# Sorting edges by one-hot products in PSUM instead of GpSimd's scatter through DRAM, in a four-layer graph network

## The chip, the cores and the metric

The kernel runs on one core of a Trainium2 chip. The metric is the time of one execution in device microseconds (us); lower is better. A profile comes from one execution of its own.

## What is computed

A graph with 3125 nodes (32 features) and 53,125 directed edges, each with a source, a destination, a type (20 of them) and 16 attributes. Four layers follow, each on the layer norm of x with a ReLU, each added to x:

```python
def reference(x, src, dst, edge_attr_16, edge_type_20, ...):
    h = relu(layernorm(x)); x = x + rel(rel(h))       # two relational layers, a relu between
    h = relu(layernorm(x)); x = x + segment_sum(h[src], dst)
    h = relu(layernorm(x)); x = x + flow(h)
    h = relu(layernorm(x)); return x + attention(h)    # softmax over each node's incoming edges

def rel(h):   # message of an edge: h[src] @ W[type], W[type] = sum of 8 basis matrices
    return segment_sum(message, dst) + h @ w_loop + bias
def flow(h):  # past = src, future = dst
    fwd = mlp_f(concat(h[future], h[past], edge_attr))   # one row for each edge
    bwd = mlp_b(concat(h[past], h[future], edge_attr))
    return mlp_n(concat(segment_sum(fwd, future), segment_sum(bwd, past)))
```

## The kernel before

**Order of the edges.** Nodes lie in 25 blocks of 128 (NB). The kernel sorts the edges by block of their destination into 440 tiles (T) of 128 slots; each tile belongs to one block, so slots stay empty at the end of a block. All layers then go over the 440 tiles.

**Sorting (sort_edges, L183 to L430)** is three blocks of code with a barrier between them. The first (L194 to L341): the edges are loaded as 125 partitions x 425 columns (EP, EC); DVE makes a mask and a running count for each block (L274 to L291), TensorE (PE) adds up counts over partitions (for which DVE waits before L291), DVE works out each edge's slot (L291 to L327). SP loads dst, src, type, then all edge attributes, then the inputs of the relation weights. GpSimd (POOL) makes constants, clears `records` and makes the weights of layer 1 (make_weights, L502 and L504). The second block (L344 to L412) goes over the 425 columns: ScalarE (ACT) copies the records of five columns to a buffer, DVE their row numbers, and GpSimd issues one indirect DMA for each column (L362), which writes 125 records of 20 floats to the DRAM tensor `sorted_edges`. Five buffers of five columns are in flight. Beside it, on the other engines, runs `table_stage` of layer 1 (L510 to L574): layer norm, 25 transposes, and for each block of nodes two products with the weights of all relations (L570) into two PSUM banks, copied by DVE (L547) and ACT (L557) and written to the table `message_table` of 62,500 rows (node, relation) by SP (L529). Two pairs of banks take turns. The third block (L414 to L430) loads `sorted_edges` back (4400 KB) and derives indices (L427 to L430).

**Relational passes.** For each of the two layers a pass goes over the tiles in steps of eight: DVE copies eight index columns (L609), GpSimd gathers eight tiles of rows from the message table (L598), DVE makes one-hot matrices, PE adds up (L630). Between them stands `table_stage` of layer 2.

**Sum layer** (sum_layer, L743) and its gathers (L798).

**Flow layer** (flow_layer, from L953). Four tiles (G) in a step, 110 steps, five buffers (BUFS), written as a loop of 22 rounds with five steps unrolled. In each step GpSimd waits for one index copy of DVE (L1017) and issues four gathers of node rows of 128 bytes (L1002); DVE makes one-hot matrices (L1019, L1024) and masked messages (L1045); ACT copies the attributes and the flag of the step's slots out of `records` into the last 17 columns of X (L1060), beside other copies; PE turns X (L1112, after it has waited for the gathers and the copy), runs the two small networks, and adds up forward (L1136) and backward messages (L1139). A step's buffer is handed back when PE is through with it.

**Attention** takes the last stretch, with 440 gathers of rows of 256 bytes (L1357); PE L1490 and ACT L1437 hand turned scores over.

## Time and profile before

| | |
|---|---|
| time, median of 3 runs | 4871.88 us (4849.11 to 4895.27) |
| span of the profiled execution | 4857.7 us |
| PE busy | 2328.2 us (48%) |
| DVE busy | 1913.1 us (39%) |
| ACT busy | 475.2 us (10%) |
| POOL busy | 2571.2 us (53%) |
| HBM read, written | 54.41 MB, 27.29 MB |

The profiled execution is one of its own: its span is the time from its first to its last instruction, and the run's time has some us around it. Busy shares are means over stages with different limits, so they say little on what sets the end; the stages have to be read one by one.

### The profile page before, as it was taken

How to read it: one execution, taken by the hardware profiler on the slowest of the kernel's cores; microseconds unless marked ns; L12 is line 12 of the kernel's file. 1: busy time of each engine (PE TensorE's matmuls, PEld its weight loads, DVE VectorE, ACT ScalarE, POOL GpSimd, SP SyncE). 2: the span in 40 equal slices, each digit the busy share in tenths (PEclk: the TensorE clock that was granted, in tenths of full speed). 3: DMA queues.
4: the chain of work that ended last, by engine and by line, in shares of the span. 5: the costliest groups of instructions: out<-in, count | busy, mean ns of one | idle time of the engine just before them, and what ended most of it. 6: DMA issues, size and time to landing. Idle time of an engine off the chain costs nothing. (4 is left out here: it accounts for less than half of the span.)

```text
span 4857.7 us, 64843 instructions
## 1 busy us (share of the span) xinstructions
PE 2328.2 (48%) x20169; PEld 1793.5 (37%) x20302; DVE 1913.1 (39%) x6164; ACT 475.2 (10%) x1072; POOL 2571.2 (53%) x2544
## 2 busy tenths in 40 slices
PE   1300002332363232335556489888888455565562
PEld 0100002333343332334555355555555344344441
DVE  8000001111121111144545466665665455555557
ACT  0000000000000000000000022222222111111110
POOL 4777775666626666644554444444443444444440
PEclk9555555555555555555656699999998556656655
DMA  3211111000020000010000100000000000000010
GB/s 89 62 7 7 7 7 48 12 11 12 11 72 12 11 11 12 12 19 14 15 15 14 12 9 8 8 8 7 8 7 5 19 15 15 16 14 16 15 15 4
DMA packets 122759, 82.94 MB, mean 17 GB/s; under 512 B 75092, under 2 KB 109016, under 8 KB 122456
## 3 DMA queue, kind: packets, MB, share of 16 engines
q0 software_dynamic: 80160, 46.17, 8.2%
q1 hardware_dynamic: 42552, 36.17, 2.6%
q8 instruction: 27, 0.44, 0.0%
q14 instruction: 20, 0.16, 0.0%
HBM read 54.41 MB, written 27.29 MB: 17 GB/s over the span
## 5 line engine op out<-in xcount | busy, mean ns | idle before, releaser
L598 POOL DMA_INDIRECT rel_rows<-message_table,rel_index x880 | 842.5, 957 | 519.0 <-issue 277.0
L630 PE MATMUL rel_acc<-rel_rows,rel_onehot 128*128 128x32 f32 x1760 | 393.6, 372 | 872.4 <-issue 582.9
L630 PEld LDWEIGHTS rel_acc<-rel_rows,rel_onehot 128*128 128x128 f32 x1760 | 402.5, 324 | 863.5 <-issue 863.2
L1002 POOL DMA_INDIRECT flow_x<-node_table,flow_index x440 | 424.6, 965 | 548.5 <-DVE flow_index L1017 440.4
L1357 POOL DMA_INDIRECT att_kv_rows<-kv_table,att_index x440 | 421.0, 957 | 508.9 <-DVE att_index L1368 380.3
L362 POOL DMA_INDIRECT sorted_edges<-scatter_rows,scatter_index x425 | 505.4, 1189 | 131.7 <-issue 128.8
L1139 PE MATMUL flow_acc_bwd<-flow_onehot_j,flow_by_q 128*128 128x309 bf16 (+1 forms) x2508 | 557.5, 337 | 8.8 <-issue 0.4
L798 POOL DMA_INDIRECT sum_rows<-node_table,sum_index x320 | 326.3, 1020 | 295.1 <-DVE sum_index L821 195.6
L609 DVE COPY rel_index<-message_indices 128x8 uint32 x110 | 22.2, 202 | 1051.7 <-remote 956.1
L860 PE MATMUL p_sum_picked<-sum_h_parts,sum_source_onehot 128*128 128x96 bf16 x3000 | 250.6, 260 | 209.7 <-issue 204.1
L831 DVE TENSOR_SCALAR sum_source_onehot<-sum_sources,sum_node_numbers 128x384 bf16<-128x384 f16 x1000 | 235.7, 314 | 289.1 <-PE p_sum_picked L860 148.8
L1393 DVE TENSOR_REDUCE att_tile_max<-p_att_scores 128x4 f32<-128x512 f32 x440 | 282.4, 685 | 95.6 <-PE p_att_scores L1502 69.8
L860 PEld LDWEIGHTS p_sum_picked<-sum_h_parts,sum_source_onehot 128*128 128x128 bf16 x3000 | 217.1, 129 | 240.4 <-issue 233.1
L663 PE MATMUL rel_acc<-w_loop,h_transposed 33*128 33x32 f32 x100 | 21.7, 398 | 578.6 <-DMA w_loop<-in_L_gnn_b 578.6
L1499 PE MATMUL p_att_scores<-att_mask,identb 128*128 128x512 bf16 x440 | 231.5, 526 | 90.8 <-ACT att_parts_turned L1437 50.2
L1502 PE MATMUL p_att_scores<-att_parts_turned,att_pick 96*128 96x128 bf16 x1760 | 238.6, 277 | 4.3 <-issue 4.2
L1136 PE MATMUL flow_acc_fwd<-flow_messages,flow_onehot 128*128 128x32 bf16 x1320 | 235.8, 179 | 8.3 <-DVE flow_by_q L1045 8.3
L663 PEld LDWEIGHTS rel_acc<-w_loop,h_transposed 33*128 33x128 f32 x100 | 21.5, 329 | 580.5 <-DMA w_loop<-in_L_gnn_b 580.5
L396 DVE COPY scatter_index<-sorted_row 125x5 uint32 (+1 forms) x85 | 14.2, 171 | 535.4 <-DMA sorted_edges<-scatter_rows,scatter_index 535.1
L1502 PEld LDWEIGHTS p_att_scores<-att_parts_turned,att_pick 96*128 96x128 bf16 x1760 | 185.2, 126 | 101.4 <-issue 81.8
L1045 DVE TENSOR_TENSOR flow_by_q<-flow_messages,source_q_mask 128x512 bf16<-128x512 bf16 x330 | 207.3, 681 | 0.0
L1024 DVE TENSOR_SCALAR flow_onehot_j<-iota_j,source_j 128x821 bf16<-128x821 f16 x440 | 199.2, 453 | 0.0
(248 smaller groups left out, 3861.8 us busy)
## 6 DMA issues: line engine op xcount, KB each, us to landing
message_table<-message_rows SPq DMA_DIRECT2D x50, 320.0 KB, 2.1
rel_rows<-message_table,rel_index POOLq DMA_INDIRECT x880
flow_x<-node_table,flow_index POOLq DMA_INDIRECT x440
att_kv_rows<-kv_table,att_index POOLq DMA_INDIRECT x440
sorted_edges<-scatter_rows,scatter_index POOLq DMA_INDIRECT x425
sum_rows<-node_table,sum_index POOLq DMA_INDIRECT x320
sorted_edges<-records SPq DMA_DIRECT2D x1, 4400.0 KB, 12.0
records<-sorted_edges SPq DMA_DIRECT2D x1, 4400.0 KB, 13.1
```

The lines of the kernel that those rows point to most:

```text
L362: pool.indirect_dma_start(out=d["sorted"], out_offset=bass.IndirectOffsetOnAxis(ap=ibuf[g][:, c:c + 1], axis=0), in_=sbuf[g][:, c, :], in_ ...
L598: pool.indirect_dma_start(out=rows[b][:, t, :], out_offset=None, in_=table, in_offset=bass.IndirectOffsetOnAxis(ap=ibuf[b][:, t:t + 1], ax ...
L630: last = pe.matmul(acc[:, bass.ds(col, F)], hot[b][:, t, :], rows[b][:, t, :], start=False, stop=True, skip_group_check=True)
L798: pool.indirect_dma_start(out=rows[b][:, t, :], out_offset=None, in_=d["nodes"], in_offset=bass.IndirectOffsetOnAxis(ap=ibuf[b][:, t:t + 1 ...
L831: last = dve.tensor_scalar(which[b % 2][:, c, :], srcs[b][:], node[:, c:c + 1], None, ALU.is_equal)
L860: last = pe.matmul(pp[b % 2][:, t * 3 * F:(t + 1) * 3 * F], which[b % 2][:, c, t * P:(t + 1) * P], top(hpart[:])[:, :, c * F:(c + 1) * F], ...
L1002: pool.indirect_dma_start(out=X[b][:, t, 0:F], out_offset=None, in_=d["nodes"], in_offset=bass.IndirectOffsetOnAxis(ap=ibuf[b][:, t:t + 1] ...
L1136: pe.matmul(accF[:, bass.ds(col(b, t), F)], hot[b][:, t, :], top(M[b][:])[:, k, t, 0:F], start=False, stop=True, skip_group_check=True)
L1139: last = pe.matmul(accB[:, lo:hi], S[b][:, t, k, :], J[b][:, t, lo:hi], start=False, stop=True, skip_group_check=True)
L1357: pool.indirect_dma_start(out=KV[b][:, t, :], out_offset=None, in_=d["kv"], in_offset=bass.IndirectOffsetOnAxis(ap=ibuf[b][:, t:t + 1], ax ...
L1393: dve.tensor_reduce(tm[b][:, 0, t, :], pR[t % PR][:].rearrange("p (h e) -> p h e", h=HEADS), AX_X, ALU.max).then_inc(max_ready, 1)
L1502: last = pe.matmul(r[:, h, :], pick[:, t * HEADS + h, :], partT[b][:], start=False, stop=True, skip_group_check=True)
```

## The change

The sort no longer goes through DRAM. The first block now also holds the whole of `table_stage` of layer 1, with one pair of PSUM banks instead of two; ACT makes its transposed copies and both halves of its output copies, and PE runs it before the counts. The edge attributes are not loaded there, and `records` and `sorted_edges` are gone. DVE makes three numbers for each edge: the source (less 1562), destination in block and type in one (less 2048), and the edge's own number, written as the bits of an f16. In the second block DVE makes, for each of the 425 columns, a one-hot row over the 440 tiles (`at`) and three rows over the 128 slots that hold the carried number at the edge's slot (`put`); PE multiplies `put` and `at` and adds up over all columns in three PSUM banks, which then hold the three numbers of each slot. 15 DVE operations decode them. Sum and flow layer read `srcf` and `valid` instead of `records`. In the flow stage GpSimd also gathers each tile's edge attributes (rows of 64 bytes) from the input by the edge number, so there are eight gathers in a step, with a second index copy on DVE; ACT copies only the flag.

```diff
-SB = 5
+SB = 4
@@ sort_edges, first block
-                    sp.dma_start(stage[:, :, 0:FE], a["edge_attr_16"].rearrange("(p c) f -> p c f", p=EP))\
-                        .then_inc(staged, 16)
                     load_weights(sp)
-                    sp.dma_start(d["sorted"].rearrange("(p t) w -> p (t w)", p=P),
-                                 s["rec"][:].rearrange("p t w -> p (t w)")).then_inc(pads, 16)
+                    front["sp"](sp)
...
-                    pool.memset(s["rec"][:], 0.0).then_inc(recs, 1)
+                    pool.iota(number[:], pattern=[[1, EC]], base=0, channel_multiplier=EC).then_inc(numbered, 1)
                     make_weights(pool)
...
+                    front["act"](act)
+                    front["dve"](dve)
...
+                    v.done(dve.tensor_scalar(carried[0][:], src[:], float(-SRC_MID), None, ALU.add))
                     v.done(dve.tensor_scalar(tmp2[:], dst[:], P - 1, None, ALU.bitwise_and))
+                    v.done(dve.scalar_tensor_tensor(out=tmp[:], in0=tmp2[:], scalar=float(TYPES), in1=typ[:],
+                                                    op0=ALU.mult, op1=ALU.add))
+                    v.done(dve.tensor_scalar(tmp2[:], tmp[:], float(DT_MID), float(-DT_MID), ALU.is_ge, ALU.add))
+                    v.done(dve.tensor_tensor(carried[1][:], tmp[:], tmp2[:], ALU.add))
...
+                    front["pe"](pe)
                     pe.wait_ge(counts_ready, 1)
@@ sort_edges, second block
+                    for j in range(EC // SG):
+                        g = j % SB
+                        if j >= SB:
+                            dve.wait_ge(used, j - SB + 1)
+                        for i in range(SG):
+                            c = j * SG + i
+                            dve.tensor_scalar(at[g][:, i, :], iotahi[0:EP, :], hi[:, c:c + 1], None, ALU.is_equal)
+                            for k in range(3):
+                                last = dve.tensor_scalar(put[g][:, i, k, :], iotalo[0:EP, :], lo[:, c:c + 1],
+                                                         carried[k][:, c:c + 1], ALU.is_equal, ALU.mult)
+                        last.then_inc(made, 1)
...
+                    for j in range(EC // SG):
+                        g = j % SB
+                        pe.wait_ge(made, j + 1)
+                        for i in range(SG):
+                            for k in range(3):
+                                last = pe.matmul(sorted_[k][:, 0:T], put[g][:, i, k, :], at[g][:, i, :],
+                                                 start=(j == 0 and i == 0), stop=(j == EC // SG - 1 and i == SG - 1))
+                        last.then_inc(used, 1)
@@ table_stage
+    deep = 1 if layer == 1 else 2
-    py = [[ps(st, f"p_message{layer}{i}{j}", [P, BANK]) for j in range(2)] for i in range(2)]
+    py = [[ps(st, f"p_message{layer}{i}{j}", [P, BANK]) for j in range(2)] for i in range(deep)]
...
         for b in range(NB):
+            if layer == 1:
+                half_out(act, act.copy, b, 0)
+            half_out(act, act.copy, b, 1)
...
-            if b >= 2:
+            if b >= deep:
                 for j in range(2):
-                    pe.wait_ge(got[j], b - 1)
+                    pe.wait_ge(got[j], b - deep + 1)
@@ flow_layer
-                            pool.wait_ge(indexed, i * BUFS + b + 1)
+                            pool.wait_ge(indexed, (i * BUFS + b) * 2 + 2)
                             for t in range(G):
                                 pool.indirect_dma_start(
                                     out=X[b][:, t, 0:F], out_offset=None, in_=d["nodes"],
...
+                                pool.indirect_dma_start(
+                                    out=X[b][:, t, 2 * F:2 * F + FE], out_offset=None, in_=a["edge_attr_16"],
+                                    in_offset=bass.IndirectOffsetOnAxis(ap=ebuf[b][:, t:t + 1], axis=0))\
+                                    .then_inc(gathered[b], 16)
...
+                        dve.tensor_copy(ebuf[b][:], s["idx_id"][:, bass.ds(g * G, G)]).then_inc(indexed, 1)
...
-                        act.copy(X[b][:, :, 2 * F:XW], s["rec"][:, bass.ds(g * G, G), 0:FE + 1]).then_inc(ea_copied, 1)
+                        act.copy(X[b][:, :, XW - 1:XW], s["valid"][:, bass.ds(g * G, G)].unsqueeze(2)).then_inc(ea_copied, 1)
...
-                        pe.wait_ge(gathered[b], i * (16 * G) + 16 * G)
+                        pe.wait_ge(gathered[b], i * (32 * G) + 32 * G)
```

## Rows read from the trace of the kernel before

**Rows 1.** The page's first line: span and instructions.
```profile
span 4857.7 us, 64843 instructions
```
**Rows 2.** Windows of scatter, relational pass, second table, flow; the header names the columns.
```profile
core 0: us, PE busy (x) PEld busy (x) DVE busy (x) ACT busy (x) POOL busy (x), PEclk, DMA share, GB/s
91.00:727.00 636.00, 58.97 (x125) 33.84 (x125) 38.58 (x127) 33.57 (x112) 505.42 (x425) 0.52 0.14 21
750.00:1386.00 636.00, 204.23 (x914) 208.02 (x914) 105.99 (x503) 0.00 (x0) 422.64 (x440) 0.50 0.10 11
1403.00:1453.00 50.00, 50.00 (x98) 31.22 (x97) 11.80 (x24) 10.22 (x24) 0.00 (x0) 0.52 0.39 151
2783.00:3740.00 957.00, 839.79 (x7136) 537.13 (x7266) 582.56 (x1754) 238.86 (x550) 424.83 (x441) 0.97 0.06 8
```
**Rows 3.** Timeline, POOL: start, duration, instruction, [idle before <- releaser]; end of scatters.
```profile
725.83 1.19 POOL L362 DMA_INDIRECT sorted_edges<-scatter_rows,scatter_index  x1 [0.30 <-issue]
...
749.51 1.04 POOL L598 DMA_INDIRECT rel_rows<-message_table,rel_index  x1 [22.49 <-DVE rel_index L609]
```
**Rows 4.** Timeline, DVE: first and third block of the sort.
```profile
4.83 6.06 DVE L274 TENSOR_SCALAR int_scratch<-dst_in 125x425 int32<-125x425 int32 x1 [4.83 <-DMA dst_in<-in_dst]
...
44.31 0.18 DVE L291 TENSOR_SCALAR total_counts<-p_counts 125x25 f32<-125x25 f32 x1
...
90.37 0.37 DVE L327 TENSOR_SCALAR dst_columns<-h_nodes 1x440 int32<-1x440 f32 x1
...
744.23 0.61 DVE L427 COPY dst_in_block<-records 128x440 f32<-128x440 f32 x1 [52.76 <-DMA records<-sorted_edges]
```
**Rows 5.** Timeline: weights of layer 1, ACT's copy, PE's products of layer 2.
```profile
67.43 1.29 POOL L502 TENSOR_TENSOR w_rel<-coef,basis 32x640 f32<-32x640 f32 x1 [55.58 <-DMA coef<-in_L_gnn_a]
...
88.32 1.52 POOL L504 TENSOR_TENSOR w_rel<-w_rel,w_rel_term 32x640 f32<-32x640 f32 x1
...
161.24 0.75 ACT L557 COPY message_rows<-p_message 128x320 f32<-128x320 f32 x2
...
1402.40 51.36 PE L570 MATMUL p_message<-w_rel,h_transposed 32*128 32x320 f32 x100 [0.76 <-DVE h_transposed L474]
```
**Rows 6.** Groups by form: xcount | busy us, mean ns of one | idle before, releasers.
```profile
L831 DVE TENSOR_SCALAR sum_source_onehot<-sum_sources,sum_node_numbers 128x384 bf16<-128x384 f16 x1000 | 235.7, 314 | 289.1 <-PE p_sum_picked L860 148.8 <-remote 129.4 <-issue 9.9
L1019 DVE TENSOR_SCALAR flow_onehot<-iota_bf,dst_in_block 128x128 bf16<-128x128 bf16 x440 | 80.7, 246 | 0.0
L277 DVE TENSOR_SCALAR block_mask<-block_of_dst 125x425 f32<-125x425 f32 x25 | 7.3, 374 | 0.0
```
**Rows 7.** Timeline, PE in the flow stage: one pair after the other.
```profile
3101.31 0.51 PE L1139 MATMUL flow_acc_bwd<-flow_onehot_j,flow_by_q 128*128 128x512 bf16 x2
...
3101.74 0.51 PE L1139 MATMUL flow_acc_bwd<-flow_onehot_j,flow_by_q 128*128 128x512 bf16 x2
```
**Rows 8.** Groups: first relational pass (750 to 1386), and flow's gathers.
```profile
L598 POOL DMA_INDIRECT rel_rows<-message_table,rel_index x440 | 423.1, 962 | 235.4 <-issue 138.8 <-DVE rel_index L609 96.6
...
L630 PE MATMUL rel_acc<-rel_rows,rel_onehot 128*128 128x32 f32 x864 | 193.5, 374 | 427.0 <-issue 276.5 <-DMA rel_rows<-message_table,rel_index 150.4
...
L1002 POOL DMA_INDIRECT flow_x<-node_table,flow_index x440 | 424.6, 965 | 548.5 <-DVE flow_index L1017 440.4 <-issue 108.0
```
**Rows 9.** Timeline, POOL: last gather of the relational pass, first and last of flow.
```profile
1384.61 0.94 POOL L598 DMA_INDIRECT rel_rows<-message_table,rel_index  x1 [0.30 <-issue]
...
2782.87 0.95 POOL L1002 DMA_INDIRECT flow_x<-node_table,flow_index  x1 [39.43 <-DVE flow_index L1017]
...
3715.54 0.99 POOL L1002 DMA_INDIRECT flow_x<-node_table,flow_index  x1 [0.30 <-issue]
```
**Rows 10.** Timeline: PE in the relational pass; PE, POOL and ACT in attention.
```profile
766.71 0.21 PE L630 MATMUL rel_acc<-rel_rows,rel_onehot 128*128 128x32 f32 x1 [2.61 <-issue]
...
4235.90 0.23 PE L1490 MATMUL p_att_parts<-identb,att_scores 128*96 128x128 bf16 x1 [0.54 <-issue]
...
4250.15 0.95 POOL L1357 DMA_INDIRECT att_kv_rows<-kv_table,att_index  x1 [0.31 <-issue]
...
4253.54 0.26 ACT L1437 COPY att_parts_turned<-p_att_parts 96x128 bf16<-96x128 bf16 x1 [17.29 <-remote]
```

251 lines of the change are left out of this document (110 added, 141 removed).

## Prediction

> **What bounds the kernel now.** I read the page first. Its span is 4857.7 us [rows 1]; the median of the runs is 4871.88, so 14.2 us lie outside the span, and I add them at the end. No engine is busy throughout, so the sum must be made by stage, with the table of windows [rows 2]. In the scatter stage (91 to 727) GpSimd (POOL) works 505.42 of 636 us and the other engines under 60 each: GpSimd bounds it. Its timeline gives the end of the stage: the last scatter is issued at 725.83, and the first gather of the relational pass goes out at 749.51, after the 4400 KB have come back (DVE's index step starts at 744.23) [rows 3, 4]. The relational pass is the second window: GpSimd's gathers bound it, with TensorE (PE) busy 204 of 636 us. In the flow stage (2783 to 3740) PE is busy 839.79 of 957 us at a granted clock of 0.97 and GpSimd only 424.83 [rows 2]: there PE bounds, and GpSimd's idle time costs nothing. The change empties the first of these stages and doubles GpSimd's work in the last, so both must be costed.
>
> **The first block after the change.** It now holds the whole message table of layer 1, which before lay beside the scatters for nothing, and nothing covers it now. It can't start before the weights are made. Before, their input waited 55.58 us, queued behind the edge attributes, and the weights were ready at 89.8 [rows 5]: from 67.43 that is 22.4 us of GpSimd work. Without the attributes in front I let the input land at about 5 us (an estimate: dst, the first load, serves DVE at 4.83 [rows 4]), so the weights are ready at about 29. Then 25 blocks. Layer 2's table does a block in 51.36 / 25 = 2.05 us of PE work, back to back [rows 5]. Now one pair of PSUM banks serves instead of two, so PE waits for the copies, and ScalarE makes both: 2.05 + 2 × 0.375 (the copy L557 takes 0.75 for two) + about 0.5 of signalling on both sides = 3.3 us. 25 × 3.3 = 83, so PE is free at 112. Only then does it run the counts products, for which DVE waits. From DVE's first read of them, L291 at 44.31, to L327's end at 90.74 it takes 46.4 us [rows 4]; this string is unchanged, so the block ends at 112 + 2 + 46.4 = 160 (before 91). DVE's eight added operations on 125 × 425 (by L427 some 0.6 each [rows 4], for 440 columns) and its norm lie in the time in which it waits for the table.
>
> **The permutation.** DVE makes 425 columns, each one row of 440 (f16, one pointer scalar) and three of 128 (two pointer scalars). The trace has no such operation in f16 exactly. Nearest for the wide one: L831, 384 columns at 235.7 / 1000 = 0.236 us; with 56 columns more about 0.25. For the narrow one: L1019, 128 columns at 80.7 / 440 = 0.183 us with one pointer [rows 6]. The second pointer is not shown; between 0 and 0.05 us of it I take 0.017, so 0.200. A column: 0.25 + 3 × 0.200 = 0.85, and 425 × 0.85 = 361 us. Bounds: 318 with narrow ones at 0.166 each, 422 at 0.247, the mean duration that L1019's records show. Should the f16 rows run like f32 rows (L277: 7.3 / 25 = 0.29 for 425 columns) it would be the same upper end. PE has 1275 products of 440 columns in this time. At full clock L1139's 512 + 309 columns recur every 0.43 us [rows 7], so 440 take 0.23 and the whole 293 us: under DVE's 361. After it 3 us for the last products, 15 decode operations at 0.65 (L427 took 0.61 for 128 × 440 [rows 4]) = 10, and 2 to start the pass: the first gather goes out at 160 + 361 + 15 = 536 instead of 749.5 [rows 3]. **Gain: 213 us.** The 4400 KB back and forth and the wait of 52.76 us on the reload are in it.
>
> **Relational pass, sum stage, attention** get the same instructions; I cost them at nothing. The copies that read the slot flags instead of the records are as many as before.
>
> **The flow stage.** GpSimd issues 880 gathers instead of 440. Before: 965 ns each [rows 8] and 0.30 between two of a run [rows 9], 1.265 us; first at 2782.87, last at 3715.54, a stretch of 932.7. Now eight belong to a step. At the clean pace 879 × 1.265 = 1112 us: GpSimd has become the bound and the stage is 179 us longer. PE's 839.79 us fit beside that, as do ScalarE's and DVE's; ScalarE's copy gets smaller, and its buffers come free with time in hand.
>
> But the clean pace holds in runs of four with a pause between them. The one place where GpSimd issues in buffers of eight with little pause is the relational pass, and there 439 gathers take 1384.61 − 749.51 = 635.1 us, 1.447 each: 962 ns of work, 138.8 us in all of its own issue and 96.6 us of waiting for the index copy on DVE [rows 8, 9], which waits for PE to free a buffer. PE is not full there (204 of 636): 276.5 us of its idle time end on nothing but "issue" [rows 8], and single products wait 2.61 us for nothing that the trace shows [rows 10]. Attention shows the same: PE ends L1490 at 4235.90, GpSimd issues gathers in a row until 4251.1, and only at 4253.54 does ScalarE's copy of that product start, after 17.29 us [rows 10]. So while GpSimd issues many gathers in a row, other engines are late to get on, and the buffers come free late. In the flow stage before, runs were short and nothing of this cost anything; after, GpSimd sets the pace. At the pace of the relational pass the 879 steps take 1272 us: **+339 us**. The bounds are 1.265 and, because the flow stage has far more PE work per buffer than the relational pass, 1.6 (an estimate: the 0.18 over the clean pace nearly doubled): +179 to +474.
>
> The Trainium skill ("Runtime: NRT & Kernel Launch", section "Instruction fetch mechanics") says that an engine fetches its instructions in blocks by its own DMA queue at a cost "mostly hidden". By that the waits above would not be of this kind, and the sum would be that of the clean pace. The trace shows waits of 17.29 us next to runs of gathers [rows 10] but not what they are.
>
> **Sum.** 4857.7 − 213 + 339 = 4984 span, plus 14.2 outside it: **4997 us**, 2.6% slower.
>
> **The rivals.**
> *B, the clean pace.* PE, DVE and ScalarE keep up and GpSimd runs at 1.265: −213 + 179 = −34, so 4824 + 14 = 4838 us, slightly faster than before. For it: flow's own gathers have this pace and waits between engines are covered by five buffers. Against it: the only long stretch of gathers on this chip's trace, 1.447. It decides if the pace in the flow stage stays under 1.265 + 34 / 879 = 1.304 us a gather: below, the kernel is faster than before; above, slower. This is the rival on the other side.
> *C, PE bounds the permutation.* Its products need the full clock. In the window 1403 to 1453 PE was busy 50.00 of 50 us, and still its granted clock was 0.52 [rows 2]: at the lower level (1.2 GHz) 1275 products take 468 (one column a cycle) to 587 us instead of 361, 107 to 226 more. With B's flow stage that gives about 4950 to 5060, with A's 5100 to 5220. The Trainium skill ("TensorE: Matmul & The Clock Gate", Part 1) has sustained matmul activity release the clock; by that C is out. The flow stage at 0.97 agrees with it, the window at 0.52 doesn't; those were f32 products, and the flow stage's bf16 are nearer to these.
> *D, GpSimd and PE take turns.* If PE gets on only while GpSimd pauses, the stage takes 839.79 + 1112 = 1952 us instead of 957: +995, in all 5650. Against it: in the relational pass PE did its work within GpSimd's.
> *E, a cheap sort.* 318 for the permutation, the table at full clock (about 27 less), flow as in B: 4838 − 43 − 27 = 4768.
>
> **How the numbers follow.** A 0.45, B 0.36, C 0.08, D 0.06, E 0.05. The predicted time is A's, 4997. The range: below it goes past B, with room for part of E, to 4780; above to 5110, a pace of 1.57 in A or C with B. D, most of C with A, and the rest of E, together under 0.2, stay out. A's own range is 4930 to 5110. What a measurement of this kernel can tell from no change is about 1% (its three runs lie 0.95% apart). Faster than 4823: E, four tenths of B, a little of A: 0.22. Slower than 4921: most of A, C, D: 0.52. Between: 0.26.
>
> **What the profile after would show.** The first gather of the relational pass near 536, the first block's end near 160 and the permutation 361 long with DVE, not PE, busy through it (C: PE busy all along, clock near 0.5). In the flow stage 880 gathers from first to last in about 1270 us with waits for the index copies of DVE (B: 1112 and none), PE with a busy share near 0.65. Wrong would be: a permutation over 422 us, from the second pointer scalar; a pace under 1.304 in the flow stage; the weights late despite the attributes being gone.

## The result

| kernel | time, median | beside it, the kernel before | ratio, 95% interval |
|---|---|---|---|
| changed | 5428.8 us | 4880.6 us | 1.115 [1.111, 1.120] |

The change makes the kernel 11.5% slower: 548 us more, where 125 us more were forecast and the range ended at 5110. The direction was right, the size was not. One more execution of the changed kernel (of four in e5 below) took 9287 us at a granted clock of 0.28; the interval of e5 leaves it out, its median does not (5413 us without it).

The page of the changed kernel: its first lines, and of its groups the gathers, PE's turning of X, and the two halves of the new sort. A group is: line, engine, operation, output<-input, count | busy us, mean ns of one | idle us before them, and what ended them.

```profile
span 5448.1 us, 68635 instructions
...
PE 2744.1 (50%) x21444; PEld 1981.2 (36%) x21577; DVE 2286.1 (42%) x7873; ACT 453.7 (8%) x1016; POOL 2503.9 (46%) x2561
...
L989 POOL DMA_INDIRECT flow_x<-node_table,flow_index x440 | 447.8, 1018 | 709.8 <-DVE flow_edge_index L1009 591.3
...
L993 POOL DMA_INDIRECT flow_x<-in_edge_attr,flow_edge_index x440 | 438.2, 996 | 145.0 <-issue 144.7
...
L1108 PE MATMUL p_x_turned<-ident,flow_x 128*81 128x128 f32 x440 | 95.5, 355 | 529.0 <-issue 521.4
...
L415 PE MATMUL p_sorted<-at_tile,put_in_slot 125*128 125x440 f16 x1275 | 253.3, 351 | 139.9 <-DVE put_in_slot L381 139.9
L381 DVE TENSOR_SCALAR put_in_slot<-iota_slot,slot_in_tile,carried 125x128 f16<-125x128 f16 x1275 | 316.3, 298 | 0.0
```

GpSimd is busy for less of the span than before, 46% against 53%, and waits 591 us for index copies in the flow stage. So GpSimd does not set the pace of this stage by its own work. PE stands idle 521 us ahead of the turning of X, for nothing that the view names.

Two windows, the permutation (the second block of the new sort) and the flow stage (columns as in [rows 2]):

```profile
161.00:562.00 401.00, 253.29 (x1275) 118.22 (x1275) 396.63 (x1720) 0.00 (x0) 0.00 (x0) 0.98 0.00 1
...
2588.00:4296.00 1708.00, 981.05 (x7002) 598.03 (x7130) 576.04 (x1842) 229.07 (x547) 885.98 (x880) 0.76 0.06 6
```

Where the time went, from the gathers in both profiled executions (from the start of the first to the end of the last):

| stretch | before | after | difference |
|---|---|---|---|
| start to first relational gather | 749.5 | 562.2 | -187.3 |
| both relational passes, first gather to last | 1339.0 | 1340.2 | +1 |
| from there to flow's first gather | 694.4 | 685.8 | -9 |
| flow's gathers, first to last | 933.7 | 1707.2 | +773.6 |
| the rest | 1141.2 | 1152.7 | +12 |

The sort is about as cheap as was forecast. All of the miss is the flow stage. Here is how it runs, from the timeline of all engines in one of its cycles:

```profile
3214.28 0.94 POOL L989 DMA_INDIRECT flow_x<-node_table,flow_index  x1 [7.69 <-DVE flow_edge_index L1009]
...
3218.44 0.20 PE L1098 MATMUL p_dst_rows<-flow_h_parts,flow_onehot_turned 128*128 x2
...
3233.03 0.94 POOL L993 DMA_INDIRECT flow_x<-in_edge_attr,flow_edge_index  x1 [0.30 <-issue]
3237.04 0.27 ACT L1064 COPY flow_x<-p_dst_rows 128x128 f32<-128x128 f32 x1 [22.19 <-remote]
...
3237.41 0.90 PE L1108 MATMUL p_x_turned<-ident,flow_x 128*81 128x128 f32 x3 [18.38 <-issue]
...
3249.03 0.95 POOL L989 DMA_INDIRECT flow_x<-node_table,flow_index  x1 [15.05 <-DVE flow_edge_index L1009]
```

GpSimd starts a run of 16 gathers at 3214.28 and ends it at 3233.97. PE ends the products of the destination rows at 3218.64, 4.4 us into the run. ScalarE's copy of exactly these products, which waits for nothing else, starts at 3237.04, 3.1 us after GpSimd has stopped. Then PE, DVE and ScalarE do two steps at their usual rhythm, hand back two buffers, and GpSimd issues the next 16.

This cycle is one of the worst. Of the nine runs of 16 that start between 3100 and 3500, each 19.7 to 21.1 us long, five go with 16 to 18 us of idle time of PE; in the other four PE is idle for 2 to 3 us from about 4.9 us after the start of the run, works on beside the gathers, and is idle for 8 to 9 us in all. Over the whole stage PE is idle for 727 us, 508 of them in 41 stretches of more than 3 us.

**What is late.** The view puts ScalarE's wait down to "remote": no instruction that makes the update ends near the time at which the update is recorded. The trace also holds the times of the semaphores' updates. The update that PE's product of 3218.64 makes is recorded at 3237.02, and ScalarE starts 0.02 us later. So ScalarE is not stopped; it is told late, and PE then waits for ScalarE. I compared every recorded update in the flow stage with the end of the last instruction before it that makes it:

| updates made by | recorded | more than 3 us late | latest |
|---|---|---|---|
| PE | 628 | 84 | 22.5 us |
| DVE | 671 | 0 | 0.04 us |
| ScalarE | 448 | 0 | 0.01 us |

Only PE's updates are late. In 39 of the 84 cases PE begins other products before the late update arrives, so what is late there is the update and not the engine. In the relational pass of the kernel before, 28 of 52 updates of PE are more than 3 us late, up to 32.5 us. Beside the scatters of the kernel before (31 updates of PE), and in the permutation (85), where GpSimd issues nothing, none is later than 0.01 us. The update behind the copy that the prediction saw in attention [rows 10] is recorded at 4253.52, 0.02 us before the copy: it is the same thing. Below it is called the freeze; in this stage it decides the time. The gathers' own packets keep moving through it (9 to 32 packets in each us from 3215 to 3235). Why PE's updates are late is not shown.

### The profile page after: what moved, and what is told of

Its sections match the earlier page's. It is cut to its first block and busy times, and to the rows that moved or that the text cites. A ratio compares the mean times of both kernels' runs of the same rounds, so it can differ in the third digit from the quotient of the medians.

```text
span 5448.1 us, 68635 instructions
## 1 busy us (share of the span) xinstructions
PE 2744.1 (50%) x21444; PEld 1981.2 (36%) x21577; DVE 2286.1 (42%) x7873; ACT 453.7 (8%) x1016; POOL 2503.9 (46%) x2561
## 5 line engine op out<-in xcount | busy, mean ns | idle before, releaser
L989 POOL DMA_INDIRECT flow_x<-node_table,flow_index x440 | 447.8, 1018 | 709.8 <-DVE flow_edge_index L1009 591.3
L1131 PE MATMUL flow_acc_bwd<-flow_onehot_j,flow_by_q 128*128 128x309 bf16 (+1 forms) x2508 | 627.8, 365 | 54.1 <-issue 46.7
L1022 DVE TENSOR_TENSOR flow_messages<-p_hidden,flow_b 128x256 f32<-128x256 f32 x110 | 46.6, 424 | 1136.4 <-PE p_hidden L1119 770.9
L993 POOL DMA_INDIRECT flow_x<-in_edge_attr,flow_edge_index x440 | 438.2, 996 | 145.0 <-issue 144.7
L784 POOL DMA_INDIRECT sum_rows<-node_table,sum_index x320 | 312.7, 977 | 309.2 <-DVE sum_index L807 211.6
L1108 PE MATMUL p_x_turned<-ident,flow_x 128*81 128x128 f32 x440 | 95.5, 355 | 529.0 <-issue 521.4
L415 PE MATMUL p_sorted<-at_tile,put_in_slot 125*128 125x440 f16 x1275 | 253.3, 351 | 139.9 <-DVE put_in_slot L381 139.9
L381 DVE TENSOR_SCALAR put_in_slot<-iota_slot,slot_in_tile,carried 125x128 f16<-125x128 f16 x1275 | 316.3, 298 | 0.0
L1108 PEld LDWEIGHTS p_x_turned<-ident,flow_x 128*81 128x81 f32 x440 | 66.5, 198 | 574.7 <-issue 573.0
```

Of the source, the lines that this page charges most:

```text
L381: last = dve.tensor_scalar(put[g][:, i, k, :], iotalo[0:EP, :], lo[:, c:c + 1], carried[k][:, c:c + 1], ALU.is_equal, ALU.mult)
L415: last = pe.matmul(sorted_[k][:, 0:T], put[g][:, i, k, :], at[g][:, i, :], start=(j == 0 and i == 0), stop=(j == EC // SG - 1 and i == SG ...
L784: pool.indirect_dma_start(out=rows[b][:, t, :], out_offset=None, in_=d["nodes"], in_offset=bass.IndirectOffsetOnAxis(ap=ibuf[b][:, t:t + 1 ...
L989: pool.indirect_dma_start(out=X[b][:, t, 0:F], out_offset=None, in_=d["nodes"], in_offset=bass.IndirectOffsetOnAxis(ap=ibuf[b][:, t:t + 1] ...
L993: pool.indirect_dma_start(out=X[b][:, t, 2 * F:2 * F + FE], out_offset=None, in_=a["edge_attr_16"], in_offset=bass.IndirectOffsetOnAxis(ap ...
L1131: last = pe.matmul(accB[:, lo:hi], S[b][:, t, k, :], J[b][:, t, lo:hi], start=False, stop=True, skip_group_check=True)
```

## Two kinds of chips

The experiments met a fact without which their numbers can't be read. On some chips the same kernel before takes about 4000 us, on others about 4880. The experiments met five chips of the quick kind and one of the slow kind. The result above is of the slow kind, on a chip whose number isn't on record. Whether it is the chip itself or something else about the machine isn't shown; one of the quick chips was met three times and was quick each time. In every comparison below the kernel before ran on the same chip as the experiment. What differs shows in the first relational pass. The groups of PE there, from the changed kernel on a quick chip:

```profile
L616 PE MATMUL rel_acc<-rel_rows,rel_onehot 128*128 128x32 f32 x864 | 195.3, 402 | 345.7 <-DMA rel_rows<-message_table,rel_index 345.7
```

On the slow chip 276.5 us of PE's idle time ended on issue and 150.4 on a DMA [rows 8]; here all of it ends on the gathered rows, and the pass's gathers follow each other at 1.26 us and not at 1.44. On the quick chips there is no freeze: of PE's 87 updates between 562 and 1200 us and 654 in the flow stage (e11) none is later than 0.01 us. It is not a difference in the fetching of instructions either: the pages of the changed kernel on both kinds show the same 37 and 32 packets on the two queues for instructions. All kernels with their results:

| label | chip kind | time | before on that chip | ratio, 95% interval | flow's gathers, first to last |
|---|---|---|---|---|---|
| e1 sort alone | quick | 3815.2 | 4002.9 | 0.954 [0.948, 0.960] | 816 |
| e2 flow alone | quick | 4385.6 | 4002.9 | 1.096 [1.089, 1.104] | 1220 |
| e3 pauses in flow | quick | 4575.7 | 4002.9 | 1.144 [1.137, 1.150] | 1592 |
| e4 memsets for attribute gathers | quick | 4361.6 | 4002.9 | 1.090 [1.084, 1.097] | 1363 |
| e5 changed kernel | slow | 5424.9 | 4884.4 | 1.109 [1.098, 1.120] | 1655 |
| e6 split | slow | 4884.8 | 4884.4 | 0.999 [0.996, 1.003] | 941 |
| e7 sort alone | quick | 3810.1 | 3990.2 | 0.954 [0.946, 0.962] | 816 |
| e8 flow alone | quick | 4372.6 | 3990.2 | 1.095 [1.084, 1.105] | 1187 |
| e9 pauses in flow | quick | 4582.0 | 3990.2 | 1.147 [1.137, 1.157] | 1593 |
| e10 few rows | quick | 4183.4 | 3990.2 | 1.047 [1.038, 1.056] | 1202 |
| e11 changed kernel | quick | 4193.1 | 3993.2 | 1.049 [1.045, 1.053] | 1212 |
| e12 pauses in flow | quick | 4577.2 | 3993.2 | 1.146 [1.144, 1.149] | 1587 |
| e13 flow alone | quick | 4379.6 | 3990.5 | 1.098 [1.093, 1.103] | 1213 |
| e14 pauses in flow | quick | 4578.2 | 3990.5 | 1.148 [1.144, 1.151] | 1589 |
| e15 second split | quick | 3973.2 | 3990.5 | 0.996 [0.994, 0.997] | 816 |
| e16, e17 pauses everywhere | quick | 4759.9, 4760.8 | 4018.7, 3990.5 | single executions | 1330, 1331 |
| e18 third split | quick | 3971.4 | 4017.0 | 0.990 [0.987, 0.994] | 817 |

## The experiments

**Is it the gathers, or does the new sort leave something behind?** The changed kernel without its attribute gathers (the attribute columns of X stay zero, so the result lacks them), and the kernel before with the same number of gathers added, by the source index and into a buffer that nothing reads.

```diff
 e1, e7 (against the changed kernel, flow_layer)
-                                pool.indirect_dma_start(
-                                    out=X[b][:, t, 2 * F:2 * F + FE], out_offset=None, in_=a["edge_attr_16"],
-                                    in_offset=bass.IndirectOffsetOnAxis(ap=ebuf[b][:, t:t + 1], axis=0))\
-                                    .then_inc(gathered[b], 16)
...
-                        dve.tensor_copy(ebuf[b][:], s["idx_id"][:, bass.ds(g * G, G)]).then_inc(indexed, 1)
...
 e2, e8, e13 (against the kernel before, flow_layer)
...
+                                pool.indirect_dma_start(
+                                    out=extra[b][:, t, :], out_offset=None, in_=a["edge_attr_16"],
+                                    in_offset=bass.IndirectOffsetOnAxis(ap=ibuf[b][:, t:t + 1], axis=0))\
+                                    .then_inc(gathered[b], 16)
...
```

> The changed kernel without the 440 attribute gathers and their index copies in the flow stage; the attribute columns of X are zero, so the edge attributes are left out of the result. Two theories. (1) The loss sits wholly in the added gathers: the flow stage is back at 933 us from first to last gather and the time is the changed kernel's 5429 less 773 = about 4656, which is 4881 less the 187 us by which the first relational gather came earlier, and some 40 less elsewhere. (2) The new sort leaves something behind (the instruction stream is longer, the buffers lie elsewhere) that slows the flow stage too: flow over 1000 us and the time over 4750.

> The kernel before, its sort untouched, with 440 extra gathers of attribute rows in the flow stage (by the source index, into a buffer that nothing reads). If the gathers alone do it: the flow stage takes 1700 us instead of 933 (1.94 us a gather) and the time is 4881 + 773 = about 5650. If the loss needs the longer chain of the change (ScalarE's smaller copy, the second index copy, scattered rows of the large attribute array): nearer to the clean pace, flow 1112, time about 5060.

Without the gathers the new sort is worth 188 us (ratio 0.954), and its flow stage takes 816 us. The kernel before was not profiled on a quick chip. But e2, which has its sort, has the first relational gather at 749.0 us there and e1 at 561.9, so the sort explains the whole difference in time; and e15 and e18, which add no gathers to the flow stage either, take 816 and 817 us for it. With the gathers alone the flow stage takes 1220. The theory that something of the sort slows the flow stage is out on these chips. The expected 1700 and 1112 for the flow stage both missed; the groups of the gathers in e11 show why it is between (below). The repeats gave the same and no slow chip:

> The changed kernel without the attribute gathers (attributes left out of the result), again, to have it on a chip where the kernel before takes 4880 us. There the flow stage should be back at 933 us and the time at 5425 - 770 = 4655, ratio 0.953, the same as on the other chip, where GpSimd's gathers did not freeze anyone. On a chip of the other kind: 3815 again.

> The kernel before with 440 extra gathers in the flow stage, again, for a chip with the freeze. If the freeze is what the long runs of gathers cost: flow stage near 1700 us instead of the 1220 of the other chip, time near 5650. If the chips differ only in the stages that were slow before: 4884 + 404 = 5290.

> The kernel before with 440 extra gathers of attribute rows in the flow stage, for a chip on which the kernel before takes 4880 us. If the whole excess of the change there (flow stage 1655 to 1707 us, against 1220 on the chips where it takes 4000) comes with the gathers, not with the new sort: flow stage near 1680 us, time 5630. If the new code around has a part in it: flow stage between 1220 and 1500.

So the split of the loss between gathers and sort is shown by e1 and e2 on quick chips only. On the slow kind the two traces carry it: the table of stretches above has 773.6 us in the flow stage and nothing elsewhere. The first split (e6, below) adds to this: on a slow chip, with the new sort and without the added gathers, the flow stage takes 941 us, against 933.7 before.

**The change itself on both kinds.**

> The changed kernel itself. In the first four runs the kernel before took 4003 us and not 4881: GpSimd's gathers of the relational passes follow each other at 1.26 us instead of 1.44 and no engine freezes beside them. If the loss of the change were the freeze alone, it would be gone here: 4003 - 187 + 179 (clean pace of 880 gathers) = 3995, no difference. From the run with the extra gathers (flow stage 1220 us instead of about 816) I expect instead 3815 + 404 = 4219, still 5% slower than before. On a chip with the freeze: 5429 again.

> The changed kernel once more. Two kinds of chips have shown: on one the kernel before takes 4880 us and the change 5425, on the other the kernel before takes 4000 and the change has not been run. By the run with 440 extra gathers (flow stage 1220 us) and the one with the new sort alone (3812) it should take 3812 + 1220 - 816 = 4216 there, ratio 1.055. On a chip of the first kind 5425 again.

5424.9 us on a slow chip, as in the result above; 4193.1 on a quick one, where 4216 were expected. The change loses on both, 540 us on the one and 200 on the other. On the quick one, GpSimd's gathers and what others waited for in the flow stage:

```profile
L993 POOL DMA_INDIRECT flow_x<-in_edge_attr,flow_edge_index x440 | 472.6, 1074 | 134.1 <-issue 133.8 <-DVE flow_edge_index L1009 0.3
L989 POOL DMA_INDIRECT flow_x<-node_table,flow_index x440 | 471.4, 1071 | 157.7 <-issue 126.8 <-DVE flow_edge_index L1009 30.9
```

```profile
L1108 PE MATMUL p_x_turned<-ident,flow_x 128*81 128x128 f32 x440 | 94.5, 350 | 294.3 <-DMA flow_x<-in_edge_attr,flow_edge_index 294.0
```

```profile
2223.00:3434.00 1211.00, 917.36 (x7176) 573.80 (x7174) 590.86 (x1848) 231.78 (x548) 943.12 (x880) 0.88 0.08 9
```

This is rival B's mechanism: GpSimd waits for nobody (31 us in all), issues 880 gathers without a pause and is the bound; PE waits for rows. Its price was too low. A gather takes 1.07 us and not 0.965 [rows 8], and with its 0.30 of issue and few waits 1.377 us on the average. The Trainium skill ("SBUF — State Buffer", section "SBUF: two separate sides") has a rule that bears on this: DVE in certain fast modes holds a port pair that GpSimd needs to write a gather's descriptors, and one waits for the other's instruction. The traces agree in part. Half of the gathers here take 0.944 us or less, as in the relational passes and in attention, but a tenth takes more than 1.25. Of the 135 gathers over 1.05 us, 124 lie beside DVE's masked messages (L1037); of the 646 under 0.96 us, 37. It is not a matter of how busy DVE is: in attention on the same chip DVE is busy for 83% of the time, against 49% here, and a gather takes 956 ns on average. No run here took L1037 away to show it.

**Does pausing help?** GpSimd got more work, a memset after each gather. In e16 and e17 the memsets stand behind the gathers of every stage, 128 x 600 in the first relational pass and 128 x 250 elsewhere.

```diff
 e3, e9, e12, e14 (against the changed kernel; idle is 128 x 600)
                                     .then_inc(gathered[b], 16)
+                                pool.wait_ge(idled, (i * BUFS + b) * 8 + 2 * t + 1)
+                                pool.sem_inc(go, 1)
+                                pool.memset(idle[:], 0.0).then_inc(idled, 1)
                                 pool.indirect_dma_start(
                                     out=X[b][:, t, 2 * F:2 * F + FE], out_offset=None, in_=a["edge_attr_16"],
...
+                                pool.wait_ge(idled, (i * BUFS + b) * 8 + 2 * t + 1 + 1)
+                                pool.sem_inc(go, 1)
+                                pool.memset(idle[:], 0.0).then_inc(idled, 1)
```

> The changed kernel with a memset of GpSimd of about 0.6 us after each of the 880 gathers of the flow stage, so GpSimd has MORE work and issues a gather each 1.95 us at most instead of each 1.25. Theory of the freeze (gathers issued back to back for more than 5 us hold up the signals to the other engines until 3 us after the last): with gaps between them nothing freezes, runs are no longer followed by waits, and the stage takes about 880 x 1.95 = 1716 us with GpSimd waiting for nothing and PE at the step's rhythm; the waits for index copies (591 us) fall under 100. Rival, the gathers' landing itself is slow (a fixed cost of 1.94 a gather for the DMA rings): same time, but PE still waits in blocks of 18 us. Rival, the freeze comes from GpSimd being busy at all: waits stay and the stage takes 1707 + 440 or more.

> The changed kernel with a memset of about 0.65 us after each of the 880 gathers, for a chip with the freeze. It took 1592 us in the flow stage on the other chip, where the stage without pauses takes about 1220. If the freeze comes from gathers issued at 1.25 us for longer than 5 us, the pauses prevent it: the stage takes about 1600, which is less than the 1655 to 1707 of the changed kernel although GpSimd works 570 us more, and no block of 18 us is left. If the freeze comes from GpSimd holding something whenever it works: the stage gets longer by the 570 us of the pauses, to 2250, the blocks get longer.

> The changed kernel with a memset of about 0.65 us after each of the 880 gathers. On a chip where the kernel before takes 4000 us: 4580 as before. On one where it takes 4880: if gathers at 1.25 us for longer than 5 us make the freeze, the pauses prevent it and the flow stage takes about 1600 us, no longer than without them (1655 to 1707), with no blocks of 18 us in which PE stands still; if GpSimd's being busy makes it, the stage takes about 2250.

> The changed kernel with a memset of about 0.65 us after each of the 880 gathers, for the same kind of chip. If what stops the other engines are gathers issued at 1.25 us for longer than 5 us, the pauses prevent it: flow stage about 1600 us, PE never idle for 18 us at a time. If it is GpSimd's being busy: about 2250 us.

> The changed kernel with a pause of GpSimd (a memset) after every gather of every stage: about 0.65 us in the first relational pass (a gather each 1.75 us at most), about 0.3 us in all others (one each 1.4). On chips where the kernel before takes 4000 us every stage gets longer: first pass 440 x 1.75 = 770 us instead of 554, second 620, sum 320 x 1.42 = 455, flow 880 x 1.42 = 1250, attention 625; in all about 4193 + 216 + 66 + 32 + 40 + 71 = 4620. On a chip where it takes 4880: if back-to-back gathers stop the other engines, the stages with short pauses come down to these same times (second pass 620 to 635, sum 455 instead of 630, flow 1250 instead of 1655, attention 625 instead of 940) and the whole to about 4700, under the 5425 of the change and even under the kernel before. If short pauses are not enough but long ones are, only the first pass loses its idle time on issue (628 us of PE in both passes). If GpSimd's being busy is what counts, all stages get longer by the pauses, over 6000 in all.

> The same kernel with pauses in every stage once more, in the hope of a chip on which the kernel before takes 4880 us. If back-to-back gathers stop the other engines, each stage with short pauses comes down to what it takes on the other chips, and the whole to about 4760, under the 5425 of the change and under the kernel before. If short pauses are not enough but long ones are, only the first pass shows no idle time of PE on issue. If GpSimd's being busy is what counts, every stage is longer than without pauses, over 6000 in all. On a chip of the other kind: 4760 again.

All six met quick chips. There the pauses cost what they add: the flow stage takes 1592 us instead of 1212, 1.81 us a gather. With a pause everywhere the first relational pass has a gather each 1.746 us, the second 1.454, attention 1.451 and flow 1.511. All of it is GpSimd at its own pace, which says once more that these chips have no freeze, and nothing on whether pauses would cure it on the others. **That question stays open.**

**Is it GpSimd's time, or its traffic?** Each attribute gather replaced by a memset of about its length (1.2 us).

```diff
 e4 (against the changed kernel; idle is 128 x 1300)
-                                pool.indirect_dma_start(
-                                    out=X[b][:, t, 2 * F:2 * F + FE], out_offset=None, in_=a["edge_attr_16"],
-                                    in_offset=bass.IndirectOffsetOnAxis(ap=ebuf[b][:, t:t + 1], axis=0))\
-                                    .then_inc(gathered[b], 16)
+                                pool.wait_ge(idled, (i * BUFS + b) * 4 + t + 1)
+                                pool.sem_inc(go, 1)
+                                pool.memset(idle[:], 0.0).then_inc(idled, 1)
...
```

> The changed kernel with each attribute gather replaced by a memset of GpSimd of about 1.1 us, so GpSimd is as long busy but issues only the 440 node gathers (the edge attributes are left out of the result). If the loss is GpSimd's time in instructions: flow stays near 1700 us. If it is the traffic that back-to-back gathers make: the node gathers are now 2.4 us apart, no blocks of frozen time, and the stage takes GpSimd's own time, about 110 x 4 x (1.26 + 1.2) = 1080 us, or PE's 933 if the memsets are shorter.

The stage took 1363 us, more than with the gathers (1212). The control was a bad one. DVE's long one-hot operations are the same in e1 and e4 and take, with the memsets beside them, three times as long. The two groups, e1 first:

```profile
L1012 DVE TENSOR_SCALAR flow_onehot_j<-iota_j,source_j 128x821 bf16<-128x821 f16 x432 | 195.5, 452 | 0.0
```

```profile
L1018 DVE TENSOR_SCALAR flow_onehot_j<-iota_j,source_j 128x821 bf16<-128x821 f16 x436 | 629.2, 1443 | 0.0
```

So a memset of GpSimd holds DVE up for longer than a gather does, and the run tells nothing on the question that it was made for; on a chip without the freeze it could not have told it in any case. The same holds, more weakly, for the pauses (DVE is busy for about 750 us of the flow stage instead of 591).

**Does a gather of fewer rows cost less?**

```diff
 e10 (against the changed kernel)
-                                    out=X[b][:, t, 2 * F:2 * F + FE], out_offset=None, in_=a["edge_attr_16"],
-                                    in_offset=bass.IndirectOffsetOnAxis(ap=ebuf[b][:, t:t + 1], axis=0))\
+                                    out=X[b][0:16, t, 2 * F:2 * F + FE], out_offset=None, in_=a["edge_attr_16"],
+                                    in_offset=bass.IndirectOffsetOnAxis(ap=ebuf[b][0:16, t:t + 1], axis=0))\
...
```

> The changed kernel with the attribute gathers cut to 16 of 128 partitions (most attributes are left out of the result): as many gather instructions, but 9/16 of the rows. If what fills up counts rows, runs of gathers can be nearly twice as long before PE stops (8 us instead of 4.7 after the start of a run), and the stage falls to about 1300. If it counts instructions, or the time in which GpSimd is at it, PE stops after the same 4.7 us and the stage keeps its 1650 to 1700 (less what the shorter instructions give).

```profile
L993 POOL DMA_INDIRECT flow_x<-in_edge_attr,flow_edge_index x440 | 439.4, 999 | 134.1 <-issue 132.2 <-DVE flow_edge_index L1011 1.8
```

16 rows take 0.999 us on average; 128 rows took 1.074 in e11, both with their delays beside DVE in them. The medians have less of these: in e10 0.852 us for 16 rows and 0.957 for the node gathers of 128. The stage is 1202 us instead of 1212, which is no clear difference (e2, e8 and e13, one kernel, take 1187 to 1220). So a gather costs by the instruction, hardly by its rows. What it says of the freeze is open, since the chip had none.

**The new sort without the added gathers.** The one-hot sort for two numbers (source, destination with type), while GpSimd, idle in it, scatters the attributes through DRAM, and reads nothing in the flow stage.

```diff
 e6 (against the changed kernel)
+def scatter(pool, s, d, first, end):
+    sent = s["moved"]["sort"]
+    for c in range(first, end):
+        j, i = divmod(c, 5)
+        if i == 0 and j >= 5:
+            pool.wait_ge(sent[j % 5], 16 * 5 * (j // 5))
+        pool.indirect_dma_start(
+            out=d["sorted"], out_offset=bass.IndirectOffsetOnAxis(ap=s["row"][:, c:c + 1], axis=0),
+            in_=s["stage"][:, c, :], in_offset=None).then_inc(sent[j % 5], 16)
...
-                            for k in range(3):
+                            for k in range(2):
...
+                @block.gpsimd
+                def _(pool):
+                    scatter(pool, s, d, SPLIT[0], SPLIT[1])
...
```

> The one-hot sort kept for the source and the destination with type, but the attributes (rows of 64 bytes) go by GpSimd's scatter through DRAM again, unrolled, straight from the loaded tile: 345 of 425 columns beside the permutation, 50 beside the second message table, 30 beside the norm ahead of the sum layer; read back ahead of the flow stage. No gather is added to the flow stage. The counts products are placed between the table's products (after blocks 8 and 10) so that DVE does not wait for the whole table. Expected: first block over at about 120 (160 before), two permutations of three: 290 us beside the scatters, the first relational gather at 120 + 345 x 1.49 + 5 = 639 (562 in the changed kernel, 749 before), flow as before. Total: 110 us under before, 3893 of 4003 (ratio 0.973). If the scatters take longer beside DVE's stream (shared port), each 1.7 us: first gather at 710, ratio 0.99.

> The one-hot sort for two numbers with the attributes scattered by GpSimd, as in the split before, with x loaded ahead of the attributes (it had waited 28 us behind them, so that the table and with it the first block ended at 170 instead of 120) and 358, 48 and 19 scatters beside the permutation, the second table and the norm. Expected: scatters from 122, the first relational gather at 122 + 358 x 1.51 + 5 = 668 (690 in the first split, 749 before), the norm ahead of the sum layer 15 us shorter than there: 65 us under the kernel before, ratio 0.986 on either kind of chip. If the scatters take the port from DVE so that the permutation ends last: it did not in the first split (437 of 520 us).

> The split version with its loads in another order: the attributes are loaded right behind x, while the table still waits for its weights (in the second split they came behind the table's first blocks, which stood still for 30 us), the zeroes behind them, and the last product of the tile map after block 21 of the table. Expected: the table over at 119 to 125 (147 there), scatters from 125 (151), the first relational gather at 125 + 360 x 1.49 + 5 = 666 (690), and the time 25 us less than the second split: ratio 0.989 to the kernel before. If it meets a chip on which the kernel before takes 4880 us: the same 0.989, and the 360 scatters issued back to back leave PE's and DVE's straight-line permutation untouched, as in the first split. If what stops PE there were any back-to-back issue of GpSimd, PE's idle time on issue in the permutation would be over 100 us.

The first split met a slow chip and made no difference there, 0.999 [0.996, 1.003]: x had come in behind the attributes, the table started late, and the first gather of the relational pass went out at 690 instead of 639. The second had the table's output wait 30 us behind the attributes' load, and its first gather also at 690. The third loads them while the table waits for its weights: first gather at 668 (666 expected), ratio 0.990 [0.987, 0.994] on a quick chip. It is quicker than the kernel before, though by 1% only: GpSimd's scatters at 1.49 us each still bound its sort.

The first split also tells something of the freeze. It ran on a slow chip, and GpSimd issued 345 scatters in one run beside the permutation. PE's group there, and a window from within it:

```profile
L436 PE MATMUL p_sorted<-at_tile,put_in_slot 125*128 125x440 f16 x850 | 174.4, 353 | 147.1 <-DVE put_in_slot L405 147.1
```

```profile
180.00:280.00 100.00, 54.87 (x270) 24.19 (x270) 100.00 (x403) 0.00 (x0) 79.59 (x68) 1.00 0.10 7
```

No idle time of PE ends on issue and DVE is busy without a gap, beside GpSimd at 79.59% with a scatter each 1.49 us. Of 75 recorded updates of PE between 180 and 600 none is later than 0.01 us. So on the slow chip a long run of GpSimd's DMA issues does not make PE's updates late by itself. The permutation differs from the stages that freeze in three things: scatters, not gathers; 1.49 and not 1.25 us between two; straight-line code on PE and DVE, not a loop whose products take their column from a register. Which of the three matters isn't shown.

## Why the prediction was wrong, step by step

**The first block** was to end at 160; it ends at 160.6, and this is partly luck. The table's blocks follow each other at 3.40 us (3.3 forecast), and DVE's first read of the counts, L303, waits for them until 119.13, 5 us later than forecast (114). The string of DVE's work behind it, taken as unchanged at 46.4 us, takes 41.5: the two errors cancel.

**The permutation** was to take 361 us; DVE takes 388, and PE's last products end 391 us after its start. The narrow operation was priced too low: within a column the wide one is followed after 0.244 us (0.25 forecast), the three narrow ones take 0.67 together, 0.223 each and not 0.200, which is within the bounds given (0.166 to 0.247). So a column costs 0.91 us. PE is busy for 0.20 us a product at a clock of 0.98 and waits for DVE: rival C is out, and the clock of the f32 window [rows 2] said nothing about f16 products. The first gather came at 562.2 instead of 536, so the gain was 187 and not 213 us.

**The stages between** were costed at nothing and cost nothing that stands clear of the scatter of single executions (-9, +1 and +12 us).

**The flow stage** is the step that failed: the price of the freeze there. The prediction saw that gathers in long runs hold up the other engines and priced this with the pace of the relational pass, 1.447 us a gather; measured are 1.94. The mechanism was right on the slow chips and the term was mis-sized: +339 us forecast, +774 measured, and the bound of 1.6 was too low as well. What was left out: in the relational pass PE has 204 us of work in 636 [rows 2] and can stand still most of the time without being missed. In the flow stage it has 840 us of work, in a chain with DVE and ScalarE in which each step needs PE's updates, so a late update soon leaves all three with nothing to do. The cycle of 34.75 us above shows it at its worst: 4.4 us of work, 18.4 us standing, 12 us of work, for two steps. That is 16.4 us of work for two steps, 8.2 a step and so close to the 8.5 of before (933.7 / 110), plus the time of standing. In such a cycle it is rival D, engines that take turns, which gives 1952 / 110 = 17.7 us a step against 17.4 here. The mean over the stage is 1707 / 110 = 15.5, between D and the forecast, since in many runs PE gets on with part of its work. The granted clock adds something: it is 0.76 over the stage instead of 0.97, and PE is busy for 981 us instead of 840. The prediction had put D aside with the remark that PE did its work within GpSimd's in the relational pass. That was the very row that could not speak for a stage with four times the work.

The prediction also said that in the flow stage before the stops cost nothing. On a quick chip this stage takes about 816 us and not 933, so over 100 us were lost there as well; PE was idle for 117 us of the window in [rows 2].

**Rival B** names the right mechanism for the quick chips, but with a gather at 1.377 instead of 1.265 us and a stage before of 816 instead of 933. The second error matters more: from 816 us, with 187 gained in the sort, the change breaks even at 1003 / 879 = 1.14 us a gather, not at 1.304. Even at the clean pace of 1.265 it would have lost: +296 us against -187. Measured are +396 in the flow stage against -187 in the sort, 4.9% slower. The forecast of "slower" was made from the freeze, but the change is slower without it too.

**Fetching of instructions**, by which the prediction thought that the waits might not be of this kind: the waits were there, and the pages show equally many packets of instructions on chips with and without them.

**A reading.** The prediction has PE end L1490 at 4235.90; that is its start, it ends at 4236.13 [rows 10]. Nothing in the sum hangs on it.

**Time outside the span**: 14.2 us were added, from the median of other executions. The execution that was profiled took 5449.94 us at a span of 5448.1, so less than 2 us lie outside.

## What to carry to other kernels

Before work is moved onto an engine that idles, ask what the others do while it works, and price a stall by their work in that stage: a stage whose other engines are a third busy hides a stop that a full one pays in whole. Gathers cost by the instruction (0.85 us for 16 rows, 0.96 for 128), so twice as many of them double GpSimd's share of the stage, however small the rows. A permutation by one-hot products runs at DVE's rate for building the matrices, here 0.91 us for 125 elements with three numbers, and leaves GpSimd free for what can run beside it. A wait that the profile ends with "issue" or "remote" is worth a look at when the semaphore's update is recorded: here it told that one engine's updates came late, where the view seemed to show engines standing still.

## What the runs showed of the hardware

- The same kernel takes 4880 us on some chips and 4000 on others. On the slow kind PE's semaphore updates come late beside runs of gathers (84 of 628 by more than 3 us in the flow stage, up to 22.5), those of DVE (671) and ScalarE (448) do not. On the quick kind none of PE's 654 is later than 0.01 us. The cause is not known.
- On the slow kind PE's updates are on time beside scatters: 345 in one run at 1.49 us with straight-line code on PE and DVE (75 updates, at most 0.01 us late).
- A gather of 16 rows takes 0.852 us in the median, of 128 rows 0.944 to 0.957; rows of 64, 128 and 256 bytes make no difference (0.944 each in e11). In the flow stage of e11 one in ten takes over 1.25 us, mostly beside one operation of DVE (L1037).
- A memset of GpSimd (128 x 1300, 1.2 us) beside DVE's one-hot operation of 821 columns lengthens that from 452 to 1443 ns.
- DVE's tensor_scalar in f16 with two pointer scalars on 128 columns repeats at 0.223 us, the one with a single pointer on 440 columns at 0.244.
- PE's f32 products back to back for 50 us (1403 to 1453 before, 50.00 us busy) had a granted clock of 0.52; f16 products at 63% busy (the permutation) had 0.98.
